# Five-stage transformer kernel on one core: one table entry in place of two matmuls, and work redrawn at three seams

## The reference, cut to what matters

```python
# stage "ac": per head, q from layer-normed x, k and v from ctx
corr = ifft(fft(q) * conj(fft(k))).real                 # over the 256 positions
w, idx = top_k(corr, 11); w = softmax(w)                # per feature
out = sum_i w_i * v[min(idx_i + pos, L - 1)]            # clamped at the last row
# stage "f0": dense layer + LoRA of one of four ranks chosen by a gate
# stage "at": 32 query heads, 8 key heads, rope, masked softmax, output projection
# stage "f1": dense layer + a Fourier-coded update of its weight
```

## Time and profile before

| | |
|---|---|
| runs | 3187.99, 3191.18, 3191.39 us; median 3191.18 |
| profiled execution | 3187.3 us, span 3185.5 us, mean granted clock 0.99 |
| PE busy | 3099.6 us (97%), 15200 matmuls |
| PE weight loads | 2592.5 us (81%) |
| DVE / ACT / POOL busy | 61% / 36% / 22% |
| DMA | 509.67 MB, mean 160 GB/s |

### The profile page before, as it was taken

The page is one execution under the profiler, slowest core; times in us unless marked ns, Lnnn a source line. Parts: engine busy times, 40 slices in busy tenths (PEclk is TensorE's granted clock), DMA queues, the critical chain, the costliest instruction groups (busy, mean ns, idle before and its releaser), DMA issues.

```text
span 3185.5 us, 42536 instructions
## 1 busy us (share of the span) xinstructions
PE 3099.6 (97%) x15200; PEld 2592.5 (81%) x15200; DVE 1946.9 (61%) x4651; ACT 1135.4 (36%) x2381; POOL 701.4 (22%) x576
## 2 busy tenths in 40 slices
PE   8999999998899899999999999999999999999999
PEld 7888788887678778888788888788888788888887
DVE  4333477777453577778666667666667666666532
ACT  4111466664122244444333333333333333333320
POOL 2422388884212123333100000000000000000131
PEclk9999999999899999999999999999999999999999
DMA  7332422113352567777564454454454455443621
GB/s 239 126 126 93 155 55 74 60 41 136 123 194 104 178 224 237 234 257 244 176 241 165 159 187 163 147 209 166 167 179 161 156 199 171 172 159 119 258 87 59
DMA packets 232877, 509.67 MB, mean 160 GB/s; under 512 B 23180, under 2 KB 58124, under 8 KB 232668
## 3 DMA queue, kind: packets, MB, share of 16 engines
q1 hardware_dynamic: 231516, 504.14, 45.9%
q10 hardware_dynamic: 1152, 2.82, 0.3%
HBM read 364.29 MB, written 142.61 MB: 159 GB/s over the span
## 4 chain that ended last, share of the span: by engine, by line
PE 65%; DVE 3%; issue 1%; ACT 1%; POOL 1%; DMA 0%; SPq 0%; DVEq 0%; POOLq 0%; ACTq 0%
PE PB L208 53%; PE PB L770 8%; PE PB L1302 3%; PE PB L741 1%; PE PB L1216 0%; ACT at_ss L1283 0%; DVE at_st L213 0%; DMA wqd<-at_wql 0%; DVE at_xt L1338 0%; DVE f0xt L794 0%; DVE at_ss L1277 0%; DVE at_ss L1294 0%; POOL at_st L217 0%; DVE at_hl L196 0%; ACT at_xr L219 0%
## 5 line engine op out<-in xcount | busy, mean ns | idle before, releaser
L208 PE MATMUL PB<-at_woh,at_ah 128*128 128x512 f32 x1024 | 411.8, 402 | 3.5 <-POOL at_wol L196 1.8
L208 PE MATMUL PB<-at_hh,at_wqh 128*128 128x512 f32 x1024 | 401.6, 392 | 0.1
L208 PE MATMUL PB<-at_hl,at_wqh 128*128 128x512 f32 x1024 | 401.2, 392 | 0.0
L208 PE MATMUL PB<-at_wol,at_ah 128*128 128x512 f32 x1024 | 400.7, 391 | 0.0
L208 PE MATMUL PB<-at_woh,at_al 128*128 128x512 f32 x1024 | 400.6, 391 | 0.0
L208 PE MATMUL PB<-at_hh,at_wql 128*128 128x512 f32 x1024 | 400.1, 391 | 0.0
L1283 ACT ACTIVATE at_ss<-at_ss,at_sm,at_bs 128x256 f32<-128x256 f32 x512 | 301.4, 590 | 270.4 <-DVE at_sm L1281 270.4
L1250 DVE TENSOR_TENSOR at_t<-PB,at_rt 128x512 f32<-128x512 f32 x128 | 88.5, 691 | 434.3 <-PE PB L208 434.3
L1338 DVE SCALAR_TENSOR_TENSOR at_xt<-PB,gt,at_xt 128x512 f32<-128x512 f32 x256 | 190.7, 746 | 115.2 <-PE PB L208 115.1
L193 ACT ACTIVATE at_ah<-PB 128x512 fp32r<-128x512 f32 x128 | 76.7, 599 | 482.3 <-PE PB L208 482.3
L208 PEld LDWEIGHTS PB<-at_woh,at_ah 128*128 128x128 f32 x1024 | 193.8, 189 | 40.5 <-POOL at_wol L196 2.0
(11 more groups left out here) (278 smaller groups left out, 7208.2 us busy)
## 6 DMA issues: line engine op xcount, KB each, us to landing
at_wqh<-wqd SPq DMA_DIRECT2D x96, 512.0 KB, 3.6
at_wql<-wqd SPq DMA_DIRECT2D x96, 512.0 KB, 4.5
at_woh<-wod SPq DMA_DIRECT2D x48, 1024.0 KB, 5.0
at_wol<-wod SPq DMA_DIRECT2D x48, 1024.0 KB, 7.4
at_rawq<-in_wq SPq DMA_DIRECT2D x32, 512.0 KB, 4.8
wqd<-at_wqh SPq DMA_DIRECT2D x32, 512.0 KB, 6.2
wqd<-at_wql SPq DMA_DIRECT2D x32, 512.0 KB, 6.9
at_rawo<-in_wo SPq DMA_DIRECT2D x32, 512.0 KB, 6.5
```

The costliest lines, as they stand in the source:

```text
L208: e.matmul(o, a, b, start=i == 0, stop=last), *(waits if i == 0 else ()), *w, mark=last)
```

## The change

**Table.** `EL` and its two matmuls per `P5` go (14 become 12). In `ck`, the table of k's forward cosine transform, the entry (last row, frequency 0) is raised by 2L, so `v[L-1]` comes in through the zero frequency. `P5(c, 1)` is cut before and after `P3` into 9 and 3 matmuls instead of 8 and 6. The last table part is 128 columns shorter.

**Begin of `f0`.** The split of the LoRA matrix moves from c = 3 to c = 6, behind `flip(2)`; its subtraction works on 64 rows, and the zeroing of the other 64 rows moves from DVE to ACT. `norm(4)` and `add_bias(2)` move from c = 6 to c = 7, behind `flip(3)` and `piece(1)`, and before `norm(5)` and `add_bias(3)`.

**Begin of `at`.** Its first two norms move from the end of tile 6 to the middle of tile 8; its third norm from the end of tile 8 to the middle of tile 10. In its first four units `weigh(u)` comes before `rest()`.

**Block ends of `at`.** w = 29: `flip(1)` moves behind `values`. w = 30: `norm(3)` comes after the first `output` instead of at the end, `values` before the second `output`, `flip(2)` at the end. w = 31: `flip(3)` after the first `output`, both projections after the second. w = 0: `turn` and the first `output` come before `scores` and `project`.

```diff
-EL = 1792 + 1536
-NTAB = EL + 128
+NTAB = 1792 + 1536
...
-    fwd = [c, s, less_last(c), oc, os, less_last(oc), less_last(os)]
+    ck = less_last(c)
+    ck[L - 1, 0] += 2 * L
+    fwd = [c, s, ck, oc, os, less_last(oc), less_last(os)]
...
-                ex = [(th[:, EL:EL + P], chh[u % 3][:, 1, :]), (th[:, EL:EL + P], cll[u % 3][:, 1, :])]
-                todo = [(a, b, ()) for a, b in ex]
+                todo = []
...
-                lo, hi = {None: (0, 14), 0: (0, 8), 1: (8, 14)}[part]
+                lo, hi = {None: (0, 12), 0: (0, 9), 1: (9, 12)}[part]
...
                 if c == 6:
-                    ahead(2)
+                    flip(2)
+                    h = op("scalar", lambda e: e.activation(bts[:, :], btr[:, :], ACT.Copy), *e_btr)
+                    l = op("vector", lambda e: e.tensor_tensor(btl[0:64, :], btr[0:64, :], asf(bts[0:64, :]), ALU.subtract), h)
+                    z = op("scalar", lambda e: e.activation(btl[64:P, :], btr[64:P, :], ACT.Copy, scale=0.0), *e_btr)
+                    e_bt += [h, l, z]
+                if c == 7:
+                    flip(3)
                     piece(1)
-                if c == 7:
-                    ahead(3)
+                    norm(4)
+                    norm(5)
+                    add_bias(2)
+                    add_bias(3)
...
-                if t == 10:
-                    yield "half"
+                if t in (8, 10):
+                    yield -t
...
-            nq[2] = norm(0, 2)
             yield
             flip(0, 1, 0, nq[1])
             flip(0, 1, 1, nq[1])
+            nq[2] = norm(0, 2)
...
+                new = w == 0 and 0 < u < NU
+                last = w == 31 and more
+                if u < NU and not new:
                     scores(u)
...
                 if u < 4:
+                    weigh(u)
                     rest()
-                    weigh(u)
...
                 if n:
                     output(n - 1, 2 * k)
+                if late:
+                    nq[3] = norm(qn + 1, 3)
+                if new:
+                    scores(u)
+                    project(u + 2)()
+                if more and w == 29:
+                    flip(qn + 1, 0, 0, nq[0])
+                    flip(qn + 1, 0, 1, nq[0])
+                    fetch_x(qn + 1, 3)
+                if last:
+                    flip(qn + 1, 3, 0, nq[3])
+                    flip(qn + 1, 3, 1, nq[3])
+                if u == NU or late:
+                    values(u - 1)
+                if n:
+                    output(n - 1, 2 * k + 1)
+                if 4 <= u < NU:
+                    weigh(u)
+                if last:
+                    project(u + 1)()
+                    load_wq(u + 3)
+                    project(u + 2)()
+                if 4 <= u < NU and not late:
+                    values(u - 1)
+                if more and w == 29:
+                    flip(qn + 1, 1, 0, nq[1])
+                    flip(qn + 1, 1, 1, nq[1])
                 if late:
                     flip(qn + 1, 2, 0, nq[2])
                     flip(qn + 1, 2, 1, nq[2])
```

More of the change, by code:

```diff
@@ L65, in dft_tables @@
         out[:, 1792 + 256 * i:1792 + 256 * i + 256] = m
-    out[P - 1, EL:EL + P] = 1.0
     return out.astype(np.float32)
@@ L590, in P5 @@
                        (sh[j], sl[j]), d["spW"][2 * j:2 * j + 2]) for j, c_ in enumerate((OEC, OES, OOC, OOS))]
-                ex = [(th[:, EL:EL + P], chh[u % 3][:, 1, :]), (th[:, EL:EL + P], cll[u % 3][:, 1, :])]
-                todo = [(a, b, ()) for a, b in ex]
+                todo = []
                 for (ah, al), (bh, bl), own in pr:
                     todo += [(ah, bh, own), (ah, bl, ()), (al, bh, ())]
-                lo, hi = {None: (0, 14), 0: (0, 8), 1: (8, 14)}[part]
+                lo, hi = {None: (0, 12), 0: (0, 9), 1: (9, 12)}[part]
                 for i in range(lo, hi):
                     a, b, w = todo[i]
-                    d["P5"] = op("tensor", lambda e, a=a, b=b, i=i: e.matmul(BK[4 + t], a, b, start=i == 0, stop=i == 13),
+                    d["P5"] = op("tensor", lambda e, a=a, b=b, i=i: e.matmul(BK[4 + t], a, b, start=i == 0, stop=i == 11),
                                  *(free[4 + t] if i == 0 else ()), *w, mark=i == hi - 1)
@@ L983, in dense @@
                     add_bias(1)
[L984 to L987, removed]
                 if c == 5:
@@ L1451, in cross_attention @@
                     fetch_x(qn + 1, 2)
-                if u < NU:
+                new = w == 0 and 0 < u < NU
+                last = w == 31 and more
+                if u < NU and not new:
                     scores(u)
-                last = w == 31 and more
-                rest = project(u + 2) if u + 2 < NU and not late and not last else None
+                rest = project(u + 2) if u + 2 < NU and not (late or last or new) else None
                 if u < 4:
+                    weigh(u)
                     rest()
-                    weigh(u)
                 if 2 <= u <= 4:
@@ L1464, in cross_attention @@
                     rest()
-                if last:
-                    flip(qn + 1, 3, 0, nq[3])
-                    flip(qn + 1, 3, 1, nq[3])
                 if n:
                     output(n - 1, 2 * k)
-                if last:
-                    project(u + 1)()
-                    load_wq(u + 3)
+                if late:
+                    nq[3] = norm(qn + 1, 3)
+                if new:
+                    scores(u)
                     project(u + 2)()
@@ L1480, in cross_attention @@
                     flip(qn + 1, 2, 1, nq[2])
[L1481 to L1491, removed]
                 split_ahead(u)
@@ L1494, in cross_attention @@
                     nq = {t: norm(qn + 1, t) for t in range(2)}
-                if more and w in (29, 30):
-                    nq[w - 27] = norm(qn + 1, w - 27)
+                if more and w == 29:
+                    nq[2] = norm(qn + 1, 2)
                 if u in (NU - 1, NU, NU + 1):
@@ L1553, in flamingo @@
                 next(at_)
-            if t == 6:
+            if t == -8:
                 next(at_)
@@ L1557, in flamingo @@
                 at_.send(q.now() + stored["w1"])
-            if t == "half":
+            if t == -10:
                 next(at_)
```

## The result

The changed kernel takes 3198.81 us (median of 8 runs, 3194.81 to 3200.08), the kernel before 3190.45 (8 runs, 3186.57 to 3194.95). The ratio is 1.0029 (95% interval 1.002 to 1.0038): 0.3% slower. The forecast was 3195.0 with a range of 3178 to 3208, "no measurable change" the likeliest at 0.40 and "slower" next at 0.35. The range held the time; the likelier of the two names did not. The change between the medians is +8.4 us, more than twice the +3.8 of the sum.

The account below looks back on a forecast made before the run. PE, busy for 97% of the span, was taken as the bound. The terms -3.8 - 6.5 + 2.0 + 1.0 + 8.5 + 2.6 = +3.8 on the profiled 3187.3, plus 3.9 to the median, gave 3195.0 us, range 3178 to 3208.

Parts of the forecast that it names:

- Part 2: Begin of `f0`: two DVE waits go, a new wait of 6 us for ACT comes; -6.5 us, bounds -4.9 and -14.
- The rival of -14: Begin of `f0` in full: PE isn't held at 800 us; -14 for -6.5, total 3187.5; chance 0.05.
- Parts 3 and 4: Begin of `at`: moved norms make later waits, +2.0 us; `weigh` first delays the split of q, +1.0 us.
- Part 1: Table: 14.5 us of PE work go, 0.48 us a pair of iterations reaches the end; -3.8 us, bounds -1 and -14.5.
- isn't shortened: From an even `P3` to the next odd one, the DVE, POOL and ACT chain making `W` sets the time, unshortened.
- Part 5: Block ends of `at`: new waits cost +1.3 at the first, +3.6 at each other, +8.5 us; new half clock +2.6.
- I take half: Half clock behind each block end's last new wait (3.0 us): 0.85 us each, +2.6 in all (0 to +5.1).
- the remainder of unit 30: At w = 0 the first `output` waits 3.0 us for it, on DVE behind the second projection's steps.
- The term for `flip(2)`: At w = 30 it takes the bank of `values(29)`, whose split on ACT stands behind `norm(3)`'s step: wait of 2.1 us.
- slower, by the clock: Rival: PE's work at block ends runs at half clock for 10 us; +8, 3203 us; slower's chance 0.35 includes longer waits.
- table in full: Rival: `W` and `ac_wtl` keep up, so the table gives -14.5 for -3.8; 3184.3 us; chance 0.10.
- Block ends as drawn: Rival: `ptl` is ready when PE gets to `values(29)`, ends cost +1 instead of +11.1; 3184.9 us; chance 0.15.

Follow-up runs that it names:

- cut7_f0_norms_late: Kernel before with P5 cut 7 and 5, the begin of `f0` as changed, and both norms and both `add_bias` called behind `lora_in(2)`: 3177.11 us, ratio 0.9968.
- before_w31_new: Kernel before with w = 31 alone reordered (`flip(3)` behind the first output, both projections behind the second): 3197.07 us against 3191.0, ratio 1.0018.
- part5_ends: Kernel before with only the new order of the block ends of `at` (w = 29 to 0): median +14.8 us.
- ends_w0_old: Kernel before with the new block ends, but w = 0 in its old order (`scores` and `project` first): 3198.96 us against 3191.0, ratio 1.0026.

## Why the prediction came out as it did

- **Part 2, the largest gain: right, and so was its successor wait.** Forecast 6.5 us less with PE at L1059's first product at 806; alone it gave 6.9 to 7.0 with PE there at 805.56, in the whole change 5.1. 1.0 of the difference is the wait for `in_four`, 2.7 against 1.7 us, and 0.5 what part 1 gives back there. The rival of -14 fell in `cut7_f0_norms_late`, which took ACT's hold away and met the transfer.
- **Parts 3 and 4: right in kind and size**, +2.0 and +1.0 forecast, +2.1 and +1.1 found. The wait in tile 8 was 4.74 us (forecast 4.95), in tile 13 1.24 (1.6).
- **Part 1: right mechanism, size too large.** 0.48 us forecast for a pair of iterations, 0.30 found, all of it from the `P3` where `W` is late to the next one, and 0.01 from there on, as forecast. Of the 0.68 us taken from behind `P3`, PE loses 0.54 to the wait for `ac_wtl` and the restart behind it (0.43 to 0.55 forecast), in every iteration, also ahead of the stretches that I had counted in full. The end of the stage gave 0.6 back, since PE only waited longer for the last unit's split (3.4 for 2.9 us). And the sentence that the chain behind `W` "isn't shortened" holds for the cut 9 and 3 alone.
- **Part 5: the step that failed, in size, is the clock behind the new waits.** The sum set the waits, the restarts and the half clock of the old ends (12.7 us at the first, 8.7 at the others) against the waits alone of the new ones, plus 0.85 us for clock ("I take half") and nothing for restarts. Half clock took 3.4 us at each of the three new ends. Found in the two traces (clock lost is the sum of (1 - PEclk) x 10 us over an end, of which up to 0.7 falls into a wait and costs nothing more; the waits at the first end leave out one of 0.8 us that both kernels have before it):

```
us at a block end                first   second   third
waits of PE, before               8.65     6.35    6.4
waits of PE after, forecast      13.95    12.35   12.35
waits of PE after, found         13.5      9.9     9.55
clock lost, before                3.4      1.7     1.7
clock lost after, forecast        0.85     0.85    0.85
clock lost after, found           3.4      3.4     3.4
longer by, forecast               2.15     4.45    4.45
longer by, found                  5.4      4.8     4.05
```

- **First end.** Its waits came to nearly the sum, so the 3.3 us that are missing are the clock (2.55) and the restarts. Inside the sum two terms were wrong and cancel. At w = 30 `at_ptl` is waited for 1.65 us instead of 4.1, PE having been held 1.8 for `at_wol` just before. At w = 0 I wrote that the first output waits for the remainder of unit 30, 3.0 us. At this end alone it waits 5.4 us for the weights `at_wol`, which are still being split there in the first block. POOL's subtraction follows a rounding that stands on ACT behind the second projection:

```profile
1549.07 1.05 ACT L193 ACTIVATE at_woh<-at_rawo 128x1024 fp32r<-128x1024 f32 x1
...
1550.20 2.35 POOL L196 TENSOR_TENSOR at_wol<-at_rawo,at_woh 128x1024 fp32r<-128x1024 f32 x1 [22.63 <-ACT at_woh L193]
```

  `scores` and `project` had covered it. I had checked the moved output's own operands at the second end only, where the weights come from memory.
- **Second and third end: right in sum, and that was luck.** 4.45 forecast with clock, 4.8 and 4.05 found. The waits were 2.45 and 2.8 us smaller than summed, the half clock 2.55 larger. Term by term at the second: `at_al` 1.07 (1.2), `at_ptl` 4.06 (4.1), `flip(2)` 0.44 (2.1), projection 1.5 (1.95), w = 0 2.8 (3.0). The term for `flip(2)` was 1.7 too large: `norm(3)`'s step came to ACT while PE still did the second output.
- **The rival "slower, by the clock"** had the side and much of the reason. It wanted 10 us at half clock at each end for 2.7 us more; about 6.8 us (two times 3.4) were found, 2.55 us more than the 0.85 summed. The shorter waits hid that at two of the ends. Its sign, PEclk below 0.8 in two neighbouring stretches, did not come: at the first two ends the half clock lay in two places, 41 and 34 us apart, and at the third in neighbouring stretches of 0.88 and 0.78. Against the sum, the profiled execution is 8.7 us longer (3199.8 for 3191.1): 3.3 from the first end, 2.3 from part 1, 1.4 from part 2 and some 1.7 from places where nothing was changed. The median is only 3.8 longer (3198.8 for 3195.0): the forecast had added 3.9 us for the quick profiled execution of before, and that of after lies 1.0 above its median.
- **The rival "table in full"** fell: no cut of `P5` that ran gave more than 6.7 of 14.5. **"Block ends as drawn"** fell too: the wait of 4.1 us stands at the second and third end of every kernel that has the whole new w = 30.

**What stays open.** Which order of a block end would beat the kernel before was not found. All five that ran were slower, and in each that was read, ACT's norm step, exponentials and two splits follow one another. The spread between executions (3191.39 to 3202.06 for `before_w31_new`) was not traced to a place.

## What to carry to other kernels

Before moving work ahead of a wait, write down for the moved instruction every operand and, for each, what stands ahead of its producer on that engine, and do it at every place where the order occurs, the first pass included: the wait of 5.4 us for weights stood at the one end where they were still being made. Then price both sides of a seam with the same terms. Here the old ends carried their restarts and half clock and the new ones hardly any, and that was the largest error of the sum. Work taken off the busiest engine pays where it stood ahead of a step that starts the next chain, and not where it was the cover of a split: the same 64 matmuls gave 2.9 us with one cut and 6.7 with another. If a wait is for a chain on another engine, moving the waiter may only change the name of the wait: `values(29)` moved back, `norm(3)` or w = 31 moved alone, `norm(4)` moved ahead and both norms moved behind were five such moves, and none gained. Only w = 0 put back gave something, since a wait of 5.4 us became one of 2.5.

## What the hardware showed that was not expected

The half clock behind equal waits falls at different places. The second and third block end of the changed kernel have the same waits (4.1, 2.8, 1.5 to 1.6 and 1.1 us). PEclk there, from 2000, 2030 and 2040 us at the second end and from 2480 and 2490 at the third (the next-to-last three columns are POOL's busy time, PEclk, DMA share):

```profile
2000.00:2010.00 10.00, 6.14 (x23) 4.83 (x23) 4.20 (x8) 5.17 (x13) 1.06 (x3) 0.83 0.00 0
...
2030.00:2040.00 10.00, 7.16 (x30) 5.76 (x29) 5.94 (x9) 2.29 (x5) 0.00 (x0) 0.85 0.77 273
2040.00:2050.00 10.00, 10.00 (x50) 8.47 (x50) 3.77 (x13) 2.45 (x8) 0.00 (x0) 0.98 0.23 81
...
2480.00:2490.00 10.00, 5.93 (x34) 4.91 (x33) 5.47 (x17) 4.99 (x12) 1.04 (x3) 0.88 0.49 182
2490.00:2500.00 10.00, 10.00 (x50) 8.53 (x49) 6.24 (x18) 2.81 (x4) 1.05 (x3) 0.78 0.00 0
```

At the second end 1.7 us are lost behind the wait of 4.1 and 1.7 behind that of 2.8; at the third 3.4, all behind the wait of 4.1 and the short ones next to it, with none behind the last. The sum over an end is 3.4 all the same, as at each end of `part5_ends`. But the sum is not fixed by the waits either: in `ends_w0_old` the second and third end have the same waits (4.1, 2.5, 1.6 and 1.1 us, and one of 0.2 or 0.4), lose 1.7 and 3.4 us to the clock, and cost 2.9 and 4.5. So a gain or loss of one such stretch is within what equal code shows, and is not to be read from one execution.
